# The last two experts' lists formed side by side, and both their gathers issued ahead of the remaining scatters

## The reference

```python
def balanced_assignment(scores):
    T, E = scores.shape
    C = T // E
    taken = jnp.zeros((T,), dtype=bool)
    parts = []
    for e in range(E):
        s = jnp.where(taken, -jnp.inf, scores[:, e])
        _, idx = jax.lax.top_k(s, C)
        parts.append(idx)
        taken = taken.at[idx].set(True)
    return jnp.concatenate(parts)
...
scores = norm @ centroids.T                         # 8192 tokens, 8 experts
sort_by_expert = balanced_assignment(scores)        # 1024 tokens each
routed = feat[sort_by_expert].reshape(E, C, D)
h = layer_norm(routed, ln_g, ln_b)
h = gelu(einsum('ecd,edf->ecf', h, w1) + b1[:, None, :])
h = einsum('ecf,efd->ecd', h, w2) + b2[:, None, :]
out = routed + h                                    # put back in the tokens' order
```

## Time and profile before

| | us |
|---|---|
| Timed runs, median of 3 (lowest, highest) | 1425.95 (1425.76, 1427.79) |
| Span of the profiled execution | 1485.4 |
| Mean granted TensorE clock in it | 0.892 of full speed |
| TensorE matmul busy | 1157.9 (78%) |
| VectorE busy | 901.1 (61%) |
| GpSimd busy | 809.1 (54%) |
| ScalarE busy | 701.1 (47%) |

### The profile page before, as it was taken

How to read it: one execution, slowest core, us unless ns; L and a number is a source line. 1 busy time by engine, 2 the same in 40 slices (tenths; PEclk the granted TensorE clock), 3 DMA queues, 4 the chain that set the end, 5 groups by cost and what they waited for, 6 DMA issues and landing times. The chain is left out here.

```text
span 1485.4 us, 33918 instructions
## 1 busy us (share of the span) xinstructions
PE 1157.9 (78%) x11356; PEld 745.3 (50%) x11356; DVE 901.1 (61%) x2806; ACT 701.1 (47%) x1485; POOL 809.1 (54%) x712
## 2 busy tenths in 40 slices
PE   0799999999999975468888680849996647888864
PEld 0244444444444433136676460739995315666743
DVE  4377767777777657787775004665556787777300
ACT  0467677676776745512223230945553722223222
POOL 0387878878788760036667751025551003667756
PEclk9999999999999997569999795869998757999977
DMA  6000000000000004403333325000000621333323
GB/s 166 8 2 0 0 0 0 0 0 0 0 0 0 1 2 129 131 20 51 50 52 66 58 25 120 0 0 1 0 0 21 173 71 26 51 66 53 56 46 28
DMA packets 82316, 54.64 MB, mean 37 GB/s; under 512 B 12865, under 2 KB 73665, under 8 KB 82241
## 3 DMA queue, kind: packets, MB, share of 16 engines
q1 hardware_dynamic: 59712, 36.89, 8.9%
q0 software_dynamic: 22528, 16.79, 8.7%
HBM read 28.49 MB, written 25.17 MB: 36 GB/s over the span
## 5 line engine op out<-in xcount | busy, mean ns | idle before, releaser
L352 POOL TENSOR_TENSOR patt_aa<-patt_aa,causal_aa 128x512 f32<-128x512 f32 x256 | 319.3, 1275 | 73.6 <-DVE patt_aa L476 71.8
L476 DVE TENSOR_TENSOR patt_aa<-p_second_aa,first_aa 128x512 f32<-128x512 f32 x384 | 247.3, 686 | 136.3 <-ACT first_aa L409 132.5
L409 ACT ACTIVATE first_aa<-p_first_aa 128x512 f32<-128x512 f32 x384 | 208.5, 596 | 139.0 <-PE p_first_aa L567 135.1
L1330 POOL DMA_INDIRECT rows_e<-norm_rows,index_e x128 | 127.3, 994 | 247.0 <-DVE index_e L1046 209.2
L567 PE MATMUL p_second_aa<-q_t_aa,k_t_aa 32*128 32x512 f32 x768 | 235.7, 642 | 0.0
L567 PE MATMUL p_first_aa<-q_t_aa,k_t_aa 32*128 32x512 f32 x768 | 217.4, 642 | 15.7 <-ACT first_aa L409 15.4
L1178 PE MATMUL p_y_e<-w_e,hid_e 128*128 128x128 f32 x1024 | 148.4, 287 | 12.7 <-issue 12.4
L586 PEld LDWEIGHTS p_z_aa<-patt_aa,v_aa 128*32 128x32 f32 x3072 | 72.4, 109 | 147.5 <-issue 80.4
L1246 PE MATMUL p_cnt_e<-reach_e,ones_e 128*128 128x240 bf16 x448 | 86.8, 324 | 75.8 <-DVE reach_e L1092 73.3
L1178 PEld LDWEIGHTS p_y_e<-w_e,hid_e 128*128 128x128 f32 x1024 | 134.1, 202 | 15.8 <-issue 15.7
L1168 PE MATMUL p_h_e<-rows_t_e,w_e 128*128 128x512 f32 x256 | 139.4, 662 | 0.1
(11 more groups left out here) (242 smaller groups left out, 2188.7 us busy)
## 6 DMA issues: line engine op xcount, KB each, us to landing
norm_rows<-norm_n SPq DMA_DIRECT2D x32, 256.0 KB, 2.4
w_e<-L_ffn_w SPq DMA_DIRECT2D x32, 256.0 KB
ffn_rows<-x SPq DMA_DIRECT2D x8, 512.0 KB, 3.2
x<-ffn_rows SPq DMA_DIRECT2D x8, 512.0 KB, 7.6
out<-x SPq DMA_DIRECT2D x8, 512.0 KB, 3.2
rows_e<-norm_rows,index_e POOLq DMA_INDIRECT x128
b_e<-L_ffn_b SPq DMA_DIRECT2D x16, 64.0 KB
ffn_rows<-yb_e,index_e POOLq DMA_INDIRECT x64
```

What stands on the lines that cost most here:

```text
L352: pool.tensor_tensor(patt[n % LAG][:, b, :, :], patt[n % LAG][:, b, :, :], causal[:, None, :].broadcast_to([P, 4, P]), ALU.mult).then_inc( ...
L409: act.activation(first[n % 2][:, b, :], p_first[b][:], ACT.Identity).then_inc(first_copied, 1)
L476: dve.tensor_tensor(patt[n % LAG][:, b, :, :].rearrange("p h q -> p (h q)"), p_second[(2 * n + b) % ROOMS][:], first[n % 2][:, b, :], ALU. ...
L1330: pool.indirect_dma_start(rows[lpar][:, j, :], None, norm_rows, bass.IndirectOffsetOnAxis(ap=list_of(l, lpar)[:, j:j + 1], axis=0)).then_i ...
```

## The change

Two places of `experts`, in both experts layers. On TensorE, in turn 7, the ranking for list 7 moves from ahead of piece 10 (the first up product) to ahead of piece 5 (the sixth down group), and the sums for list 7 from ahead of piece 14 (the fifth up product) to ahead of piece 11 (the second). On GpSimd, turn 7 issues gather 6, gather 7 and then the two halves of scatter 4; before, the scatter came first. The other turns keep their order, and VectorE's, ScalarE's and SyncE's programs aren't edited.

```diff
@@ TensorE, turn 7
-                            if lists and n == 10:
+                            if lists and n == 5:
                                 rank_chosen(E - 1, (E - 1) % 2)
-                            if lists and n == 14:
+                            if lists and n == 11:
                                 for q in range(CHUNKS // 2):
                                     list_chunk(E - 1, q)
                                 list_fold(E - 1)
@@ GpSimd
                 def turn(e, par, half):
                     _, lists, compute = does(e)
+                    last = len(lists) > 1
+                    for l in lists if last else ():
+                        gather(l, l % 2)
                     if compute and (not isinstance(e, int) or e > 2):
                         for h in range(2):
                             scatter(e - 3, 1 - par, half, h)
-                    if lists:
+                    if lists and not last:
                         gather(lists[0], 1 - par)
-                    for l in lists[1:]:
-                        gather(l, par)
                     if isinstance(e, int) and e == E + 1:
                         for h in range(2):
                             scatter(e - 2, par, half, h)
```

## The result

The changed kernel takes 1429.54 us (median of 14 runs) against 1427.05 for the kernel before (14 runs): a ratio of 1.0016, 95% interval 1.0009 to 1.0023, so 1.3 to 3.3 us more. The forecast was 1427.5 on the 1425.95 known then, 1.6 us more, with 1.0011 as ratio. The range held the time, the sign was that of the sum, and most of this chapter is about why the sum's terms were not all the right ones.

What follows compares the result with a forecast made beforehand. It took the timed kernel to be bound by GpSimd from gather 5 to the end. Terms +0.6 and +0.2 gave +0.8 us a stage, +1.6 for two stages on 1425.95: 1427.5 us, range 1407 to 1433.

Steps and rivals of the forecast that it cites:

- nameless stalls: Waits behind gathers put down to an unknown queue; claimed absent from timed runs, 17.6 us in the second experts stage.
- stalls real and shrinking: Rival: stalls also in timed runs, shrinking in the new order; 1399 to 1423 us, middle 1412.5; chance 0.26.
- (a): Ahead of gather 6: GpSimd waits for list 6, a loss of 0.6 us a stage, bounds 0 and 3.4.
- (b): List 7 earlier on TensorE: gather 7 starts without a wait; TensorE about 1 us earlier, taken at nothing.
- the rival in which TensorE bounds the tail: TensorE bounds the timed tail after all: gains 2 to 3 us in all, 1423 us; chance 0.08.
- The cover on TensorE: Before scatter 7: TensorE's work ready 2.2 us before GpSimd comes to it, 2 us earlier still after the change.
- (c): Scatters 4 and 5 move 20 us back: no cost, the copies hide it with 5 us and more.
- (d): Gather 6 runs beside VectorE's work for list 7: net loss 0.2 us a stage, bounds 0 and 0.4.
- The slower rival: GpSimd idles for list 6 ahead of gather 6: 4.3 us a stage, 8.6 in all, 1434.5 us; chance 0.14.

Runs made afterwards that it cites:

- second profile: The kernel before, unchanged, timed and profiled again: span 1424.7 us, ratio to the kernel before 1.0002.
- list 6 early: The changed kernel with list 6 summed one down group earlier on TensorE: ratio to the kernel before 1.0010.
- Order alone: The changed kernel with list 7 ranked and summed where it stood before, so only GpSimd's order changes: ratio to the kernel before 1.0060.
- odd profile: The first profiled execution of the kernel before, unchanged: span 1485.4 us, against a timed median of 1425.95.
- list 6 late: The changed kernel with list 6 summed two down groups later on TensorE, list 7's ranking also later: ratio to the kernel before 1.0043.
- lists alone: The kernel before with only TensorE's part of the change, list 7 ranked and summed earlier: ratio to the kernel before 0.9994.
- half first: The changed kernel with one half of scatter 4 put back ahead of the two gathers: ratio to the kernel before 0.9993.
- gather 7 later: The kernel before with gather 7 moved behind the first half of scatter 5: ratio to the kernel before 1.0008.

## Why the prediction was right, and where it wasn't

**What binds the kernel.** Right, and it was the step that mattered. The prediction took the nameless stalls for a property of the profiled execution, on the argument that 59.5 us lay between the span and the timed median, and computed GpSimd's row without them. The second profile shows that row, 90.3 and 90.7 us long against 89.75 on paper. The rival that would have made the kernel faster (stalls real and shrinking, 0.26) falls with it: the span fell by 59 us as that rival's profile would, and the timed median didn't follow. Had the forecast been made from the chain of waits alone, it would have promised 27 us.

**(a) The gap ahead of gather 6.** Forecast a loss of 0.6 us, measured 1.18 - 0.30 = 0.88, in both stages. That is the sum's first mis-sized term. Its two parts were off in opposite ways. The list came sooner than thought, 0.40 us behind gather 5's last issue (1338.46 against 1338.06) where 0.65 was worked out. But from the finished index to the first issue it takes 0.78 us (1338.46 to 1339.24), not the 0.2 that the prediction set without a row for it. The kernel with list 6 early confirms the price.

**(b) List 7 in time for gather 7.** Right: index 7 at 1347.90, gather 7 could start at 1349.51. The spare time is 1.6 us less the 0.78 of the step above, close to the 0.65 worked out. Measured from gather 5's first issue the index comes 4.4 us earlier than in the second profile of before (19.9 against 24.3), not 5 to 6. Order alone shows what it is worth, 3.6 us a stage. TensorE reaches expert 5's down products 26.8 us behind gather 5's first issue instead of 27.9 (1354.77 and 1354.62 less their starts), the 1 us that was forecast, and it earns nothing: GpSimd has no gap ahead of any scatter, before or after, so the rival in which TensorE bounds the tail (1423) is out too. The cover on TensorE wasn't put to the proof by a run of its own.

**(c) Scatters 4 and 5 later.** No cost, as forecast, but with less cover than was said: scatter 4's last issue ends at 1374.17, its rows land 1.8 us later, and expert 6's copy is at 1377.34. That is 1.4 us, not 5. The copy's row still names TensorE as what it waited for:

```profile
1377.34 0.60 ACT L1305 ACTIVATE yb_e<-p_y_e 128x512 f32<-128x512 f32 x1 [3.78 <-PE p_y_e L1178]
```

**(d) GpSimd's issues beside VectorE's list work.** Wrong in sign. The prediction charged gather 6 with 0.3 us and credited scatter 4 with 0.1, from the odd profile, in which scatter 4 had slid away from the marks. In the second profile scatter 4 takes 15.46 and 15.71 us in the two stages where an undisturbed one takes 14.97 (the fence with 2.02, 1.69 and 1.71), and gather 6 takes 10.28 in the changed kernel where it took 10.08 before. So the change wins 0.3 and 0.5 us in the two stages here, and scatters 5 to 7 together take another 0.1 and 0.3 us less, for which no row gives a reason. The section of the Trainium skill that the prediction weighed (SBUF — State Buffer, Who interferes with whom) speaks of VectorE instructions in a two-port mode, which block GpSimd for their whole length; of tensor_tensor, which the marks are, the same section says that it contends with GpSimd's reads alone and was not seen to stall DMAs. The traces bear out neither a full block nor none: single issues of 2.02, 2.39, 2.60 and 2.68 us stand beside list work, those of 2.02 and 2.39 overlap no VectorE instruction but tensor_tensor, and others beside the same marks take 0.94 or 1.55. The Trainium skill's example of a five-fold DMA doesn't fit: over a whole expert the toll was never above 1.6 us (the gather with the issue of 2.39 us, 11.54 against 9.98). No run separated the port from other causes; that the slow issues lie beside the list work is shown, why is open.

**What the sum lacked.** The drain. Of the 1.9 us between the spans of before (second profile) and after, the tails carry 0.5 + 0.1 and the drains 0.66 + 0.65. The stages' other parts differ by up to 1.1 us each way between these two profiles and happen to cancel, so the fit to 0.1 us is partly luck:

| term, both stages, us | forecast | measured |
|---|---|---|
| gap ahead of gather 6 | +1.2 | +1.8 |
| issues beside VectorE's marks, and rest of the tail | +0.4 | -1.2 |
| drain at the stage's end | not seen | +1.3 |
| sum | +1.6 | +1.9 (timed: 1.3 to 3.3) |

The timed runs bear the drain out, roughly. The four kernels with the drain of 4.63 us (changed, order alone, list 6 late and early) are by the centres 1.7, 1.1, -0.2 and 2.0 us slower than their tails alone would have them, 1.2 on average, where two drains are 1.3 us longer; the three with a shorter drain and turn 6 as before (lists alone, half first, gather 7 later) by 0.0, -0.2 and 0.8. Each of these has an error of a microsecond or more, so this supports the drain's price and doesn't prove it.

So the number was right partly by two errors that cancel: the sum put the end of the stage at nothing, where the drain took 1.3 us more, and it put the issues at a loss of 0.4, where they won 1.2. A reader who repeated this sum for another order would have missed by the drain: the version with list 6 early, where the tails say 0.6 us less than before, is 1.4 us slower by the centres.

**The slower rival**, a list so late that GpSimd stands idle 3.4 us, didn't come about, but its mechanism was the right one at a quarter of the size, and list 6 late shows it at the full size: 1.0043, where the prediction's 8.6 us would be 1.0060, and 1.0048 with only its 3.4 us a stage for list 6 counted.

## What to carry to other kernels

Where one engine issues without a pause, the order of its work is worth only the waits that it makes or takes away: before putting an urgent item first, look whether it is ready at that moment and what would fill the time until then. Compare the span of a profile with the timed median before trusting its longest waits; if the span is some per cent longer, profile the same kernel a second time, for waits without a named releaser may be that execution's alone. And count the end of a stage, its drain and barrier, among the things that an order can change.

## What the runs showed of the hardware that was not expected

GpSimd's drain instruction at a stage's end takes about 4 us, though the last scatter's rows have landed by the time it starts (the last completion comes 1.6 to 1.8 us behind the last issue's end, the drain begins at 1.9 to 2.1). It took 3.97 us with 20 or 24 scatters behind the last gather, 4.14 with 28 and 4.63 with 32, within 0.01 us in all kernels and both stages. It is on the path: in the first stage SyncE issues the next load 6.87 us behind the last scatter's end before the change and 7.48 after it, some 0.85 us behind the drain's end in both.

From a finished index, and just so from a finished copy of ScalarE (1336.80 to 1337.63, 1344.78 to 1345.57), to GpSimd's first dependent DMA it is 0.8 us when the engine stands waiting, and nothing above the usual 0.30 when the index had been there for 1.6 us (gather 7 in the changed kernel).

A single indirect DMA of 128 rows can take 2.4 us instead of 0.94 to issue, or 2.7 instead of 1.55, beside VectorE's list work. What decides whether it does isn't its place against the marks: in "list 6 late" the fifth issue of gather 6 begins 1.20 us behind the first mark in both stages, and takes 2.39 us in the first and 1.03 in the second. Between the two stages of this one execution it made 1.3 us, more than half of what the whole change costs by the centres.
